# First attention's output projection as three single-pass products over high and low parts, and the scaling of batches moved to GpSimd

## The reference

```python
attn = softmax(scores)                                  # 16 heads, 1601 keys
ctx_c = einsum('bhsl,bld->bhsd', attn, kv_r)            # 64 columns a head
ctx_lat = einsum('bhsd,hkd->bhsk', ctx_c, w_kc_kv)
ctx = ctx_lat.transpose(0, 2, 1, 3).reshape(B, S, H * K)
x = x + ctx @ Wo.T
# then, of the feed-forward block, per batch:
weights = layernorm(x) @ W_r + b_r
topk_vals, topk_idx = top_k(weights, 64)
```

## Time and profile before

| | us |
|---|---|
| median of 3 runs | 1634.17 |
| the profiled execution, whole | 1630.33 |
| its span | 1628.5 |
| attention of layer 0 ends, this phase begins | 1141.4 |
| first residual addition (L1582) | 1153.65 |
| last residual addition of the loop | 1217.43 |
| first feed-forward product (L1787) | 1228.27 |

### The profile page before, as it was taken

The page is one execution under the profiler, slowest core; times in us unless marked ns, Lnnn a source line. Parts: engine busy times, 40 slices in busy tenths (PEclk is TensorE's granted clock), DMA queues, the critical chain, the costliest instruction groups (busy, mean ns, idle before and its releaser), DMA issues. The chain is left out here.

```text
span 1628.5 us, 49586 instructions
## 1 busy us (share of the span) xinstructions
PE 1555.9 (96%) x16244; PEld 1269.8 (78%) x16244; DVE 1291.7 (79%) x3021; ACT 1055.8 (65%) x2158; POOL 1150.2 (71%) x1097
## 2 busy tenths in 40 slices
PE   5879999999999999999999999998999899999998
PEld 4658888888888888888888888887886455555887
DVE  6988888888888888898888888886783678885223
ACT  5877777777777777777777777776232466664121
POOL 5439999999999999999999999999200224431321
PEclk8699999999999999999999999999999999999999
DMA  9731121122122122112112113510940011101344
GB/s 258 243 89 50 47 84 40 49 72 62 48 59 72 40 59 74 48 47 84 40 55 76 48 53 90 111 48 26 220 86 1 7 42 66 66 8 54 102 150 162
DMA packets 181917, 123.65 MB, mean 76 GB/s; under 512 B 106651, under 2 KB 169225, under 8 KB 181473
## 3 DMA queue, kind: packets, MB, share of 16 engines
q1 hardware_dynamic: 180320, 118.90, 26.5%
q0 software_dynamic: 1536, 3.99, 0.7%
HBM read 81.06 MB, written 24.48 MB: 65 GB/s over the span
## 5 line engine op out<-in xcount | busy, mean ns | idle before, releaser
L1308 POOL TENSOR_TENSOR c_rest<-c_prob 128x1024 f16<-128x1024 f32 (+1 forms) x512 | 814.8, 1608 | 37.5 <-ACT c_prob L1052 17.3
L1052 ACT ACTIVATE c_prob<-c_psS,ln,c_exp_scale 128x1024 f32<-128x1024 f32 (+1 forms) x512 | 526.4, 1041 | 144.8 <-PE c_psS L823 141.3
L1188 DVE TENSOR_REDUCE c_mxp<-c_psM 128x1 f32<-128x400 f32 (+1 forms) x1024 | 569.5, 572 | 59.4 <-PE c_psM L807 40.2
L823 PE MATMUL c_psS<-c_q,c_kk 128*128 128x256 f16 (+1 forms) x3328 | 509.3, 273 | 1.6 <-ACT c_prob L1052 0.8
L841 PE MATMUL c_psV<-c_vb,c_prob 128*128 128x129 f16 (+1 forms) x3328 | 419.5, 221 | 3.1 <-POOL c_rest L1308 2.0
L844 PE MATMUL c_psV<-c_vb,c_rest 128*128 128x65 f16 (+1 forms) x3328 | 393.6, 193 | 0.0
L823 PEld LDWEIGHTS c_psS<-c_q,c_kk 128*128 128x128 f16 (+1 forms) x3328 | 308.9, 99 | 67.2 <-ACT c_prob L1052 1.2
L807 PE MATMUL c_psM<-c_kkm,c_q 128*128 128x400 f16 (+1 forms) x1024 | 341.7, 334 | 4.1 <-DVE c_mxp L1188 2.9
L841 PEld LDWEIGHTS c_psV<-c_vb,c_prob 128*128 128x128 bf16 (+1 forms) x3328 | 312.4, 98 | 16.2 <-POOL c_rest L1308 2.5
L844 PEld LDWEIGHTS c_psV<-c_vb,c_rest 128*128 128x128 f16 (+1 forms) x3328 | 302.9, 98 | 28.3
L2296 ACT ACTIVATE g_prob<-g_psS,g_bias 128x128 f32<-128x128 f32 (+1 forms) x256 | 104.1, 427 | 50.9 <-DVE g_bias L2346 50.9
(11 more groups left out here) (338 smaller groups left out, 2434.8 us busy)
## 6 DMA issues: line engine op xcount, KB each, us to landing
c_w2s<-w_scr SPq DMA_DIRECT2D x65, 256.0 KB, 2.6
c_ms<-m_scr SPq DMA_DIRECT2D x65, 192.0 KB, 2.7
c_w2s<-w_scr SPq DMA_DIRECT2D x64, 128.0 KB, 2.0
acc_scr<-c_acc SPq DMA_DIRECT2D x128, 64.0 KB, 2.0
kv<-acc_scr SPq DMA_DIRECT2D x16, 512.0 KB, 7.3
m_w<-in_L_ffn_W SPq DMA_DIRECT2D x16, 352.0 KB, 3.6
c_vb<-V SPq DMA_DIRECT2D x24, 129.0 KB, 2.0
kv<-in_ctx SPq DMA_DIRECT2D x8, 384.0 KB
```

Source lines behind the costliest of these rows:

```text
L823: mm = pe.matmul(psS[g % 2][0:r, i * S:(i + 1) * S], src[:, (lo + i) * P:(lo + i) * P + r], mov[slot][:, :], start=(one == 0 and i % 2 == ...
L1052: nc.scalar.activation(prob[g][0:r, 0:w], psS[g % 2][0:r, 0:w], ACT.Exp, bias=keep["ln1024"][0:r, :], scale=exp_scale[slot][0:r, :]).then_ ...
L1188: nc.vector.tensor_reduce(mxp[:, st, c:c + 1], psM[:, st, 0:CHUNKS[c][1]], AX.X, ALU.max).then_inc(mx_done, 1)
L1308: nc.gpsimd.tensor_tensor(rest[g][0:r, 0:w], prob[g][0:r, 0:w], high[0:r, 0:w], ALU.subtract).then_inc(rest_done, 1)
```

## The change

It does two things. The output projection is computed from high and low parts in the type float32r: `cT` becomes the high part of the transposed sums (ScalarE's copy writes float32r), VectorE computes what it lost (`c_low`, four instructions of 512 columns a batch, straight from the PSUM bank); `wvo` is split in the same way once at the start, the high part by ScalarE and the low part by VectorE. `project` accumulates high x high, high x low and low x high, 24 matmuls in place of 8. And the scaling of batches 1 to 7 is issued by GpSimd, ahead of its clears, in place of VectorE. TensorE's transposes of the next batch now wait for `low_done`, the low part, where they waited for the copy. `c_low` and the weight parts use the SBUF space of `pickT`, `xgT` and `hT`, which are written later. The reciprocal of the denominators is issued in two pieces. In the attention phase one semaphore is merged into another.

```diff
@@ phase_attention0, GpSimd
-            nc.gpsimd.memset(acc[1][:], 0.0).then_inc(acc_zeroed, 1)
+            nc.gpsimd.memset(acc[1][:], 0.0).then_inc(filled, 1)
...
-            pool.wait_ge(acc_zeroed, 1)
+            pool.wait_ge(filled, 3)
@@ phase_project0_ffn0
-    cT = [sb(f"cT{i}", [P, G, P]) for i in range(2)]
+    cT = [sb(f"cT{i}", [P, G, P], F32R) for i in range(2)]
...
+        c_low = [parts.enter_context(nc.sbuf_tensor(f"e_c_low{i}", [P, G, P], F32R)) for i in range(2)]
...
+    W_HALVES = 2
...
+        w_parts = parts.enter_context(nc.sbuf_tensor("e_w_parts", [P, 2, G, D], F32R))
+    w_high, w_low = w_parts[:, 0], w_parts[:, 1]
@@ GpSimd
         def _(pool):
+            for b in range(1, B):
+                pool.wait_ge(inverted, min(b, 2))
+                scale_batch(pool, nc.gpsimd, b)
             for u in range(2):
                 nc.gpsimd.memset(ahead["vm"][u][:], 0.0).then_inc(ahead["vm_zeroed"], 1)
@@ VectorE
+            def columns_low(b, s):
+                for half in range(2):
+                    dve.wait_ge(t_done, W_HALVES + 4 * b + 2 * s + half + 1)
+                    part = slice(4 * half, 4 * half + 4)
+                    nc.vector.scalar_tensor_tensor(
+                        out=c_low[s][:, part].rearrange("p g c -> p (g c)"), in0=psT[2 * s + half][:],
+                        scalar=keep["k_unscale"][:, 0:1], in1=cT[s][:, part].rearrange("p g c -> p (g c)").bitcast(F32),
+                        op0=ALU.mult, op1=ALU.subtract).then_inc(low_done, 1)
...
-            later = keep["rec"][:, H0 + 1:B * H0 + 1, :]
-            nc.vector.reciprocal(later, later).then_inc(inverted, 1)
+            for lo, hi in ((1, 2), (2, B)):
+                later = keep["rec"][:, lo * H0 + 1:hi * H0 + 1, :]
+                nc.vector.reciprocal(later, later).then_inc(inverted, 1)
+                if lo == 1:
+                    for k in range(W_HALVES):
+                        dve.wait_ge(t_done, k + 1)
+                        part = slice(k * G // W_HALVES, (k + 1) * G // W_HALVES)
+                        nc.vector.tensor_tensor(w_low[:, part], wvo[:, part], w_high[:, part].bitcast(F32),
+                                                ALU.subtract).then_inc(low_done, 1)
+                    columns_low(0, 0)
+            columns_low(0, 1)
             dve.wait_ge(ones_made, 2)
-            dve.wait_ge(inverted, 1)
             dve.wait_ge(in_c, 80)
             for b in range(B):
-                if b + 1 < B:
-                    scale_batch(dve, nc.vector, b + 1)
                 add_rows(b)
                 if b > 0:
                     choose(b - 1)
+                if b + 1 < B:
+                    columns_low(b + 1, 0)
                 statistics(b)
                 raw_logits(b)
                 logits(b)
+                if b + 1 < B:
+                    columns_low(b + 1, 1)
                 select(b)
@@ TensorE, turn
-                            pe.wait_ge(t_done, 4 * (b - 1) + 2 * s + half + 1)
+                            pe.wait_ge(low_done, W_HALVES + 4 * (b - 1) + 2 * s + half + 1)
@@ TensorE, project
-                pe.wait_ge(t_done, 4 * b + 2 * s + 2)
+                pe.wait_ge(t_done, W_HALVES + 4 * b + 2 * s + 2)
...
                 for g in range(G):
-                    mm = pe.matmul(psO[s][:, 0:D], cT[s][:, g, :], wvo[:, g, :], start=(g == 0), stop=(g == G - 1))
+                    pe.matmul(psO[s][:, 0:D], cT[s][:, g, :], w_high[:, g, :], start=(g == 0), stop=False)
+                if b == 0:
+                    pe.wait_ge(low_done, W_HALVES)
+                for g in range(G):
+                    pe.matmul(psO[s][:, 0:D], cT[s][:, g, :], w_low[:, g, :], start=False, stop=False)
+                pe.wait_ge(low_done, W_HALVES + 4 * b + 2 * s + 2)
+                for g in range(G):
+                    mm = pe.matmul(psO[s][:, 0:D], c_low[s][:, g, :], w_high[:, g, :], start=False, stop=(g == G - 1))
                 mm.then_inc(o_full, 1)
@@ ScalarE
+            act.wait_ge(keep["in_wvo"], 16)
+            for k in range(W_HALVES):
+                part = slice(k * G // W_HALVES, (k + 1) * G // W_HALVES)
+                nc.scalar.activation(w_high[:, part], wvo[:, part], ACT.Copy).then_inc(t_done, 1)
             act.wait_ge(eps_made, 2)
```

More of the change, by code:

```diff
@@ L12 @@
 F32 = mybir.dt.float32
+F32R = mybir.dt.float32r
 F16 = mybir.dt.float16
@@ L594, in phase_attention0 @@
     zeroed, filled = sem("c_zeroed"), sem("kk2_filled")
-    acc_zeroed, summed, inverted = sem("acc_zeroed"), sem("summed"), sem("inverted")
+    summed, inverted = sem("summed"), sem("inverted")
     v_ones, v_high, v_low = sem("v_ones"), sem("v_high"), sem("v_low")
@@ L1495, in phase_project0_ffn0 @@
     pick = sb("pick", [P, NT, P])
+    with ExitStack() as parts:
+        c_low = [parts.enter_context(nc.sbuf_tensor(f"e_c_low{i}", [P, G, P], F32R)) for i in range(2)]
     pickT = sb("pickT", [P, NT, P])
+    W_HALVES = 2
     xgT = sb("xgT", [P, DK, NSEL])
+    with ExitStack() as parts:
+        w_parts = parts.enter_context(nc.sbuf_tensor("e_w_parts", [P, 2, G, D], F32R))
+    w_high, w_low = w_parts[:, 0], w_parts[:, 1]
     hT = sb("hT", [P, FT, NSEL])
@@ L1505, in phase_project0_ffn0 @@
     ones_made, eps_made, inverted = sem("ones_made"), sem("eps_made"), sem("inverted")
+    low_done = sem("low_done")
     t_full, t_done, o_full, o_done = sem("t_full"), sem("t_done"), sem("o_full"), sem("o_done")
```

## The result

The changed kernel takes 1660.21 us (median; 1658.47 to 1662.43) against 1633.84 for the kernel before: a ratio of 1.0159, 95% interval 1.0147 to 1.017. The forecast was 1646, the range 1633 to 1658. The sign and the mechanism held; the size did not.

The account below looks back on a forecast made before the run. TensorE bounds the stage, VectorE just behind and the bound after the change. Profiled 1630.33 us + 1.1 (VectorE's intervals) + 10.8 (GpSimd holds) = 1642.2; the median stands 3.84 higher, so 1646, range 1633 to 1658.

Parts of the forecast that it names:

- The projection: Output projection: a float32r matmul every 0.115 us, TensorE needing 7.9 us a batch, so it is not the bound.
- Rival (b): In the projection, a float32r matmul takes longer than one pass or waits for its weights: 1660 us, chance 0.10.
- VectorE at the old pace: VectorE's work per batch: 9.29 us, making it the bound; first and last intervals together add 1.1 us.
- The scaling on GpSimd: GpSimd's scaling of batches 2 to 7 holds VectorE instructions for 1.8 us a batch, +10.8 us.
- The clears: GpSimd's clears, 7.82 us, moved behind all scalings: cost nothing by themselves.
- rival (c): The moved clears hold VectorE too, between 0 and 7.8 us; at 4 on top 1650 us, chance 0.15.
- The head: Start of the stage: added weight and low-part work ends before x is loaded; nothing, at most 2 us if uncovered.

Follow-up runs that it names:

- experiment 1: The changed kernel with GpSimd's two clears put behind the last gather of selected rows; 1653.69 us, ratio 1.011.
- experiment 10: The changed kernel with GpSimd's two clears moved back ahead of the scalings; 1652.31 us, ratio 1.0104.
- experiment 2: As experiment 1, with the scaling of batches 1 to 7 left out altogether; 1635.02 us, ratio 1.0004.
- experiment 6: As experiment 2, but GpSimd issues a clear of 2304 columns of idle vm buffers in place of each scaling instruction; 1643.83 us, ratio 1.0057.

## Why the prediction was wrong in size

- *The projection* (0.115 us a matmul, so that TensorE is no bound): 0.117 at the full clock, right. Rival (b) is dead.
- *VectorE at the old pace* (9.29 us): 9.05 to 9.10, right; `columns_low` comes 0.66 from start to start (1183.02, then the statistics at 1184.34 behind two), where 0.70 was priced. The step's +1.1 us was 0.1.
- *The scaling on GpSimd* (1.8 us a batch, +10.8): the mechanism and the held kinds were right. In the changed kernel the holds of batches 2 to 7 sum to 13.2, 2.2 a batch: the term was too small by 2.4 us. Batches 4 and 6 do what was forecast, the first scaling holding the end of `select` (`e_gate` 1.76) and the second the pick (`e_pick` 1.18), but at a cost of 2.35 us a batch. In 3 and 5 the second scaling alone holds, 1.4 to 1.6. Two batches fall outside the forecast's pattern: in 2, ahead of any steady state, each scaling held a product, 3.38 together; in 7 both met the end of `select`, the first `e_selb`, the second `e_sel`.
- *The clears* ("nothing by themselves"): this step failed, and with it the sum. A tensor_scalar caught in the scaling ahead of them stood over both. The clears cost 7.85 us in the profile, 6.5 by experiment 1, 7.9 by experiment 10. It was rival (c), at 4 us and a chance of 0.15, with the full 7.8 as its bound. The reason against it was L518 passing beside the clears: two inputs, so it spoke only for its own kind.
- *The head* ("nothing, at most 2 us if that cover fails"): the cover held for the first residual addition and failed behind it. `w_low` and the scaling of batch 1 stand in each other's way (5.65 in place of 2.36). The first addition still waits for the load of x, 1.69 where it waited 5.08, and comes 11.7 us after the last memset in both kernels. The second tile's projection is late: VectorE waits 0.70 for it and 0.74 for the next columns. Where `w_low` took 2.36 (experiments 2, 6 and 10), the two additions follow each other without a wait.
- *Not in the forecast at all*: TensorE's idle times were expected, but not that it comes back from some of them at the 1.2 GHz level (after 1.82 us before 1187.51, after 7.33 under the long hold), eight matmuls 1.91 for 1.10. The waits of VectorE for TensorE and ScalarE, the 0.70 and 0.74 of the head included, are 3.2 us. How much of them is the clock was not separated.

The sum with these terms in place is 1630.33 + 0.1 + 13.2 + 7.85 + 3.2 = 1654.7 for the profiled execution of before; its median stands 3.5 higher, at 1658.2. The last 2 us of the 1660.21 lie outside the stage and are not explained.

## What to carry to other kernels

Before work goes to GpSimd to relieve VectorE, list VectorE's instructions by kind. In these runs, beside GpSimd's arithmetic on SBUF the two-input ones and the tensor_scalars stood to its end; beside its memsets only the tensor_scalars did; those with an input in PSUM (two `columns_low` in 1.40 us, as always) and the statistics (two in 0.74) passed. What helped was to start each GpSimd instruction by a semaphore where VectorE reads PSUM (12.6 us less than experiment 1), to cut it into short ones (10.9 less), and, against the changed kernel, to put memsets where VectorE has two-input work (7.9 less) or behind the whole stage (6.5 less) rather than directly behind arithmetic. And this stage, whose bound and second engine lie half a microsecond apart, gave nothing for the relief of one.

## What the runs showed of the hardware

- A tensor_scalar caught in a GpSimd tensor_tensor is let in at the boundary to another tensor_tensor (1.89, then 1.82 for the next instruction), but was not at the boundary to a clear that followed without a wait, nor at any boundary between the clears behind: 9.65 us over three instructions, 10.21 over seventeen, one case each. With one semaphore wait in between it ended after 1.89, again in one case. A tensor_scalar first caught in a clear was let in at that clear's end (2.70, 2.00). What decides this inside the chip no run shows.
- Holding is mutual: two scalings of 3.8 us took 4.76 beside two subtractions on VectorE, in quarters 6.61 instead of 4.83.
- A tensor_scalar of 128x1 was not held beside a clear (0.45 us for two), those of 128x2 were (2.70, 2.00).
